# State space layer: head products and transposes issued singly between the wide products, and a new order of the steps around them

## The chip, the cores and the metric

The kernel runs on one core of one Trainium2 chip. The metric is the device time of one execution in microseconds (us); lower is better. The engines are TensorE (PE in the profile; PEld is its weight load), VectorE (DVE), ScalarE (ACT), GpSimd (POOL) and the DMA queue of SyncE (SP).

## The reference, cut to what matters

Four layers with residuals and layer norms around them: causal attention, a gated FFN, a state space layer (the subject here), a second gated FFN. The state space layer has a batch of 2 rows of 1024 tokens, width 512, 64 heads of 64 channels in 8 groups, and a state of 128 per channel:

```python
gate = proj[..., :I]; hbc = proj[..., I:I + CONV_DIM]; dt = proj[..., -H:]
xBC = silu(causal_conv4(hbc) + conv_bias)           # x, B, C
dA = exp(dt_p * A); dtx = dt_p[..., None] * x
state = state * dA + dtx * B_t;  y_t = state . C_t   # a scan over the tokens
y = y + x * D
yn = y * rsqrt(mean_group(y * y) + EPS) * norm_weight * silu(gate)
out = yn @ out_proj_w
```

## The kernel before, in words

The rows of the batch are a hardware loop over b. In it the phases attention, projection, FFN, time steps, state space (MAMBA in the code), FFN follow one another. The state space phase goes over 8 groups g of 8 heads each (`m_group`, one for each engine; the groups 1 to 6 are a hardware loop), and in a group over 8 chunks c of 128 tokens: 128 iterations `it` in all. The scan is done in chunks: within a chunk with products against a 128x128 decay matrix for each head, across chunks with a carried state. Each engine has its order written out by hand, and semaphores tie them together: an engine works strictly in its own order.

Every float32 operand of a large product is split into a high and a low part, and three products of the parts are added ("wide" products: 12 of 128x128 weights by 512 columns for each 128x512 output; helper `three`, L591 to L593; `features` is the projection of x, B, C for the convolution, `tokens` the gate's). Products of unsplit float32 (the heads', the state's) are two passes each.

TensorE's order in one iteration (L946 to L1017), with its bank in PSUM:

1. the four transposes of x for this chunk into bank 2 (L956), after `yt_ready` and `x_tm_ready` of the iteration before; ScalarE copies them to `x_tm` (L1239);
2. B's transpose and the product C by B into bank 3 (L961, L962). Bank 3 is also the out projection's, so these wait for `mo_used`: VectorE has added the last out projection to Y (`gather`, L1675, or L1673 for the first group);
3. the decays' sums, 4 products of 512 columns into banks 4 and 5 (L939, L940);
4. none, one or two projections for later chunks or the next group, 12 wide products each, into bank 0 or 1 in turn (even c: two; odd c: one; the last group has none from c = 4). Behind the first one stand the four transposes of the previous iteration's result yn into bank 2 (`turn_out`, L922);
5. the gate's projection, 12 wide, into the other of banks 0 and 1 (`bank_read` waits until that bank's last content was read by VectorE: `conv_ready`, signalled at L1647, for a projection);
6. the state's product into bank 6 (L997);
7. the 8 heads' products, decay matrix by xdt, 64 columns each, 2 passes: 16 in a row, into bank 7 (L1004), after `m_ready`, `pool_x`, `ss_ready`;
8. the out projection of the previous iteration into bank 3, 12 wide (`project_out`, L925), after `yt_ready`;
9. the update of the state, B by xw, into bank 6 (L1017), not for c = 7.

VectorE's order (L1696 to L1748): the masked decay matrix (L1659, L1662); for each projection the convolution's three taps (L1643, and for the second half of the tokens three small ones with the carry, L1640); after the first one yt_lo, the low part of the transposed result, which signals `yt_ready` (L1667); silu's product (L1652); the gate's product g_th (L1719); y's two additions (L1726 adds the heads' products from bank 7, L1729 adds the skip term xd and signals `y_ready`); at c = 1 and 6 the copies of `tables` (L1684, L1686); `gather` (L1675); the state's addition (L1744); the final yn (L1746).

ScalarE's order (L1234 to L1290): x_tm, b_tm, the decays' exp (L1218), for each projection the convolution's first tap (L1203) and silu's tanh (L1208), yt_hi behind the first (L1213), splits of weights, the gate's tanh (L1268), the eight scaled reads of bank 6 into yv (L1274), the square with its sum (L1277), splits of weights.

GpSimd's order (L2012 to L2059): xdt, xw, xd, splits of weights (L1993), the state's decay (L2032, after `inter_done` of the state's product), the two masked tables for the next chunk (L1999), the root (L2044, L2046), splits of weights.

Of the kernel before, what the change touches and what calls it, by code (L numbers as in the profile page):

```python
# [64 lines left out]
def build(nc, x, w_attn, qk_bias, bv, bo, w_ffn0, lr0, lr0_const, w_ffn1,  # L65
          w_mamba, w_dt, conv_par, dt_bias, a_log, d_skip, out):
    ctx = ExitStack()
    with ctx:
# [182 lines left out]
        pool_x = sem("pool_x")  # L251
# [334 lines left out]
        def _(pe):  # L586
# [173 lines left out]
            with pe.Fori(0, B) as b:  # L760
# [158 lines left out]
                def turn_out(it):  # L919
                    pe.wait_ge(yn_ready, START + it + 1)  # L920
                    for k in range(XT):
                        r = pe.transpose(bank[2][:, k * P:(k + 1) * P], yn[:, k * P:(k + 1) * P], ident[:])  # L922
                    r.then_inc(yt_done, 1)

                def project_out(it):  # L925
                    pe.wait_ge(yt_ready, START + it + 1)
                    for k in range(XT):
                        r = three(bank[3][:], lambda q: yt_hi[:, q, :], lambda q: yt_lo[:, q, :],
                                  lambda q: wy_hi[:, q, :], lambda q: wy_lo[:, q, :], k, k == 0, k == XT - 1)
                    r.then_inc(mo_done, 1)  # L930
# [12 lines left out]
                def m_group(g, first, last):  # L943
                    uses = m_uses(last)
                    at = 0
                    for c in range(TT):  # L946
# [5 lines left out]

                        pe.wait_ge(yt_ready, START + (it if start else it - 1))
                        pe.wait_ge(x_tm_ready, START + it)
                        for k in range(XT):
                            r = pe.transpose(bank[2][:, k * P:(k + 1) * P], xbc[s][:, k, ck], ident[:])  # L956
                        r.then_inc(xtr_done, 1)
# [9 lines left out]
                        turned = start  # L967
                        while uses[at][0] == "proj":
                            n = uses[at][1]
                            bank_read(g, at, uses)  # L970
                            ft = n % CT
                            if n < CT:
                                features(bank[at % 2][:], wx_hi[:, ft, :], wx_lo[:, ft, :], 1).then_inc(proj_done, 1)
                            else:
                                pe.wait_ge(m_split, b * (MG * W_PER_G) + (g + 1) * W_PER_G + (ft + 1))
                                features(bank[at % 2][:], wx_hi[:, ft, :], wx_lo[:, ft, :], 0).then_inc(proj_done, 1)
                            at += 1
                            if not turned:
                                pe.wait_ge(x_tm_ready, START + it + 1)
                                turn_out(it - 1)  # L980
                                turned = True
                        if start:
                            decays(it)
                        if not turned:
                            pe.wait_ge(x_tm_ready, START + it + 1)
                            turn_out(it - 1)

                        bank_read(g, at, uses)
                        if c == 0:
                            pe.wait_ge(m_split, b * (MG * W_PER_G) + g * W_PER_G + (CT + KT))  # L990
                        tokens(bank[at % 2][:], c, wg_hi, wg_lo).then_inc(gate_done, 1)
                        at += 1
# [14 lines left out]
                        if not start:  # L1007
# [37 lines left out]
                turn_out((b + 1) * (MG * TT) - 1)  # L1045
                norm_turn(b * 4 + 3, 3, (2, 3))
                project_out((b + 1) * (MG * TT) - 1)
# [7 lines left out]
        def _(act):  # L1055
# [87 lines left out]
            with act.Fori(0, B) as b:  # L1143
# [77 lines left out]
                def m_group(g, first, last):  # L1221
# [12 lines left out]
                    for c in range(TT):  # L1234
# [34 lines left out]
                        at += 1  # L1269
# [5 lines left out]
                        r.then_inc(inter_used, 1)  # L1275
                        act.wait_ge(y_ready, START + it + 1)
# [78 lines left out]
        def _(dve):  # L1355
# [170 lines left out]
            with dve.Fori(0, B) as b:  # L1526
# [161 lines left out]
                def m_group(g, first, last):  # L1688
# [7 lines left out]
                    for c in range(TT):  # L1696
# [27 lines left out]
                        dve.wait_ge(inter_used, START + it + 1)  # L1724
                        dve.wait_ge(intra_done, START + it + 1)
                        dve.tensor_tensor(yv[:], yv[:], bank[7], ALU.add)  # L1726
                        dve.drain()
                        dve.wait_ge(pool_x, START + it + 1)
                        dve.tensor_tensor(yv[:], yv[:], xd[:], ALU.add).then_inc(y_ready, 1)  # L1729
# [433 lines left out]
```

## Time and profile before

| | us |
|---|---|
| median of 3 runs (4126.3 to 4149.99) | 4126.65 |
| the profiled execution | 4139.81 |
| its span in the trace | 4138.1 |
| TensorE busy in the span | 3813.2 (92%) |
| VectorE busy | 2753.9 (67%) |
| ScalarE, GpSimd busy | 1706.8, 1816.2 |
| mean granted TensorE clock | 0.932 |

The times of the trace are us from the start of the span. A timeline's line is: start, duration, engine, line of the code, operation, what it writes and reads, count; in brackets the engine's idle time before it and what ended it. TensorE's records overlap (a product is recorded until its result is in PSUM), so its pace is read from one start to the next, not from the durations.

### The profile page before, as it was taken

What the parts mean: (1) busy time and instruction counts of PE and PEld (TensorE: products, weight loads), DVE (VectorE), ACT (ScalarE), POOL (GpSimd) and SP (SyncE); (2) the same over time, 40 slices, a digit from 0 to 9 for tenths busy, and PEclk for the clock granted to TensorE, in tenths of its full rate; (3) what the DMA queues carried; (4) which work ended last, traced back from release to release, by engine and by line L of the source; (5) the groups of instructions that cost most, each with busy time, mean ns of one, the idle gap of its engine ahead of it and who ended that gap; (6) DMA issues with size and microseconds to landing.
All of it is one profiled execution on the core that took longest, in us unless ns stands there. A gap on an engine that the chain in (4) does not pass through costs nothing.

```text
span 4138.1 us, 61540 instructions
## 1 busy us (share of the span) xinstructions
PE 3813.2 (92%) x18088; PEld 2789.9 (67%) x18088; DVE 2753.9 (67%) x5102; ACT 1706.8 (41%) x3555; POOL 1816.2 (44%) x1977
## 2 busy tenths in 40 slices
PE   7899899799999999979889998997999999999797
PEld 5444588577777777767654446875777777777676
DVE  5657455677777777764655655556777777777645
ACT  1434411455555555541214443114555555555412
POOL 1111444266655665553211124433565555655532
PEclk9867899899999999999987868998999999999998
DMA  3221111101010011011132111111011100110111
GB/s 81 47 35 23 63 45 33 33 26 37 28 33 20 26 36 28 23 36 54 38 68 44 32 50 34 46 32 39 21 37 33 28 26 20 36 33 18 47 43 36
DMA packets 84630, 151.95 MB, mean 37 GB/s; under 512 B 16488, under 2 KB 18616, under 8 KB 84432
## 3 DMA queue, kind: packets, MB, share of 16 engines
q1 hardware_dynamic: 82320, 145.38, 13.3%
q10 hardware_dynamic: 2112, 4.19, 0.3%
q8 instruction: 92, 1.51, 0.2%
q14 instruction: 106, 0.87, 0.1%
HBM read 119.37 MB, written 4.19 MB: 30 GB/s over the span
## 4 chain that ended last, share of the span: by engine, by line
PE 71%; issue 8%; DVE 8%; ACT 4%; DVEq 2%; POOL 2%; POOLq 1%; DMA 1%; SPq 1%; ACTq 1%; PEldq 0%; PEld 0%
PE banks L591 16%; PE banks L592 15%; PE banks L593 15%; PE banks L1004 4%; PE banks L841 4%; PE banks L822 3%; PE banks L799 3%; PE banks L997 2%; DVE conv L1643 2%; PE banks L1017 2%; DVEq L1646 1%; PE banks L939 1%; PE banks L940 1%; ACT conv L1203 1%; DVE conv L1640 1%
## 5 line engine op out<-in xcount | busy, mean ns | idle before, releaser
L1643 DVE SCALAR_TENSOR_TENSOR conv<-banks,cpar,conv 128x509 f32<-128x509 f32 (+2 forms) x576 | 428.6, 744 | 113.4 <-ACT conv L1203 98.3
L1169 ACT ACTIVATE probs<-banks 128x1024 f32<-128x1024 f32 (+3 forms) x384 | 298.7, 810 | 282.4 <-PE banks L822 281.4
L1967 POOL TENSOR_SCALAR_AFFINE_SELECT probs<-probs 128x256 f32<-128x256 f32 x256 | 104.3, 408 | 664.8 <-ACT probs L1169 664.4
L1430 DVE TENSOR_TENSOR Y<-banks,Y 128x512 f32<-128x512 f32 x368 | 253.3, 691 | 160.6 <-PE banks L593 160.1
L2032 POOL TENSOR_TENSOR state<-state,gt 128x512 f32<-128x512 f32 x112 | 133.5, 1192 | 505.4 <-PE banks L997 505.4
L591 PE MATMUL banks<-xhi,f_hi 128*128 128x512 f32 x800 | 325.0, 406 | 30.9 <-POOL f_lo L1846 16.6
L799 PE MATMUL banks<-stack_k,stack_q 48*128 48x512 f32 (+3 forms) x768 | 299.1, 466 | 39.0 <-DVE mx L1563 9.7
L591 PE MATMUL banks<-xhi,wx_hi 128*128 128x512 f32 x768 | 314.2, 409 | 6.8 <-DVE conv L1643 6.6
L592 PE MATMUL banks<-xhi,f_lo 128*128 128x512 f32 x800 | 320.3, 400 | 0.0
L593 PE MATMUL banks<-xlo,f_hi 128*128 128x512 f32 x800 | 320.2, 400 | 0.0
L592 PE MATMUL banks<-xhi,wx_lo 128*128 128x512 f32 x768 | 308.1, 401 | 0.0
L593 PE MATMUL banks<-xlo,wx_hi 128*128 128x512 f32 x768 | 307.8, 401 | 0.0
L1004 PEld LDWEIGHTS banks<-xdt,decay 128*128 128x128 f32 x2048 | 248.4, 192 | 68.6 <-issue 68.6
L1558 DVE CUSTOM_DVE_ANT_0 banks<-banks,mask_qk 128x128 f32<-128x128 f32 (+3 forms) x512 | 248.2, 501 | 64.8 <-PE banks L799 60.9
L822 PE MATMUL banks<-stack_q,stack_k 50*128 50x512 f32 (+3 forms) x768 | 272.4, 456 | 9.1 <-DMA stack_q<-mt_lo 7.7
L591 PE MATMUL banks<-wg_hi,xhi 128*128 128x512 f32 x512 | 221.8, 433 | 45.2 <-DVE conv L1643 41.9
L822 PEld LDWEIGHTS banks<-stack_q,stack_k 50*128 50x128 f32 x768 | 156.6, 232 | 153.9 <-issue 116.2
L1004 PE MATMUL banks<-xdt,decay 128*128 128x64 f32 x2048 | 242.8, 272 | 5.2 <-issue 2.6
L1844 POOL TENSOR_SCALAR f_hi<-f_raw 128x512 fp32r<-128x512 f32 x150 | 96.9, 646 | 321.9 <-PE banks L593 299.8
L1274 ACT ACTIVATE yv<-banks,gt 128x64 f32<-128x64 f32 x1024 | 223.8, 332 | 25.2 <-PE banks L997 25.2
L799 PEld LDWEIGHTS banks<-stack_k,stack_q 48*128 48x128 f32 x768 | 151.8, 221 | 121.0 <-DVE mx L1563 48.6
L1100 ACT CAST h_hi<-hf 128x512 fp32r<-128x512 f32 x100 | 62.3, 623 | 408.3 <-DVE hf L1415 408.3
(219 smaller groups left out, 10134.6 us busy)
## 6 DMA issues: line engine op xcount, KB each, us to landing
m_raw<-in_w_mamba SPq DMA_DIRECT2D x224, 256.0 KB, 2.6
f_raw<-in_w_ffn SPq DMA_DIRECT2D x50, 768.0 KB, 4.6
x_next<-in_x SPq DMA_DIRECT2D x6, 1024.0 KB, 8.6
stack_q<-X SPq DMA_DIRECT2D x96, 64.0 KB, 2.4
stack_k<-X SPq DMA_DIRECT2D x96, 64.0 KB, 2.5
wqk_raw<-in_w_attn SPq DMA_DIRECT2D x8, 512.0 KB, 3.5
stack_q<-part_hi SPq DMA_DIRECT2D x64, 64.0 KB, 2.4
stack_k<-part_hi SPq DMA_DIRECT2D x64, 64.0 KB, 2.5
```

The source lines that it names most:

```text
L591: pe.matmul(dst, a_hi(kt), w_hi(kt), start=first, stop=False)
L592: pe.matmul(dst, a_lo(kt), w_hi(kt), start=False, stop=False)
L593: return pe.matmul(dst, a_hi(kt), w_lo(kt), start=False, stop=last)
L799: pe.matmul(bank[RING_BANK[use]][:, 0:cols], stack_q[buf][base:base + ROWS, h, i * P:(i + 1) * P], stack_k[buf][base:base + ROWS, h, s * H ...
L822: r = pe.matmul(bank[h][:, at:at + w], stack_k[buf][base:base + ROWS + 2, h, j * P:(j + 1) * P], stack_q[buf][base:base + ROWS + 2, h, s * ...
L841: r = pe.matmul(bank[6][32 * h:32 * h + VW, lo:HALF], V[:, j, QUAD * t + h, :], probs[n % 2][:, h, at:at + w], start=j == 0, stop=j == CPH ...
L1004: r = pe.matmul(bank[7][:, h * MP:(h + 1) * MP], decay[:, h, :], xdt[:, h * MP:(h + 1) * MP], start=True, stop=True, skip_group_check=True)
L1169: act.activation(probs[n % 2][:, 2 * p:2 * p + 2, 0:w], banks[:, 2 * p:2 * p + 2, 0:w], ACT.Exp, scale=1.0 / HD ** 0.5).then_inc(exp_done[ ...
L1274: r = act.activation(yv[:, own], bank[6][:, own], ACT.Identity, scale=gt[:, EC, c, h:h + 1])
L1430: dve.tensor_tensor(Y[:, i, :], bank[6 + i % 2], Y[:, i, :], ALU.add).then_inc(f["dn_used"], 1)
L1558: dve.tensor_tensor_reduce(out=src, in0=src, in1=mask_qk[:, HALF - cols:HALF], scale=1.0, scalar=NEG, op0=ALU.add, op1=ALU.max, accum_out= ...
L1643: r = dve.scalar_tensor_tensor(out=rest, in0=src[:, 0:HALF - lag], scalar=cpar[:, o:o + 1], in1=rest, op0=ALU.mult, op1=ALU.add)
```

## The change

On TensorE:

- The heads' products are no longer a block of 16. They stand singly in the out projection: behind each of its wide products 0 to 7 one head (two passes).
- The four transposes of x for the next chunk stand behind wide products 8 to 11 of the out projection, where the next chunk is in the same half of the tokens ((c + 1) % 4 is not 0); otherwise, and for the first two chunks of the first group, they stay at the head of the iteration.
- The four transposes of yn stand behind wide products 8 to 11 of the first projection of the iteration, not behind the whole of it; without a projection (last group, c of 4 and more) behind products 0 to 3 of the gate's.
- The state's product (L997) is issued ahead of the gate's projection, not behind it.
- The heads wait for the new `xdt_ready` (xdt alone), and `pool_x` (xdt, xw and xd) is waited for by the state's update.

On ScalarE the eight reads into yv go ahead of the gate's tanh. On VectorE y's two additions go ahead of the gate's product, and a drain stands before yn. GpSimd signals `xdt_ready` behind xdt.

```diff
+                def wide(dst, a_hi, a_lo, w_hi, w_lo, between):
+                    n = 0
+                    for kt in range(KT):
+                        for a, w in ((a_hi, w_hi), (a_lo, w_hi), (a_hi, w_lo)):
+                            r = pe.matmul(dst, a(kt), w(kt), start=n == 0, stop=n == 3 * KT - 1)
+                            if n == 3 * KT - 1:
+                                r.then_inc(between["done"], 1)
+                            if n in between:
+                                between[n]()
+                            n += 1
+                def head(it, h):
+                    if h == 0:
+                        pe.wait_ge(m_ready, it + 1)
+                        pe.wait_ge(xdt_ready, it + 1)
+                        pe.wait_ge(ss_ready, START + it)
+                    r = pe.matmul(bank[7][:, h * MP:(h + 1) * MP], decay[:, h, :], xdt[:, h * MP:(h + 1) * MP],
+                                  start=True, stop=True, skip_group_check=True)
+                    if h == HPG - 1:
+                        r.then_inc(intra_done, 1)
...
-                        for k in range(XT):
-                            r = pe.transpose(bank[2][:, k * P:(k + 1) * P], xbc[s][:, k, ck], ident[:])
-                        r.then_inc(xtr_done, 1)
+                        if c % CPH == 0 or first and c == 1:
+                            pe.wait_ge(yt_ready, START + (it if start else it - 1))
+                            for k in range(XT):
+                                turn_x(it, c, k)
...
+                        turning = {} if start else {8 + k: lambda k=k: turn_out(it - 1, k) for k in range(XT)}
...
+                        bank_read(g, at, uses)
+                        heads = {h: lambda h=h: head(it, h) for h in range(HPG)}
+                        early = {n - 8: turn for n, turn in turning.items()}
+                        wide(bank[at % 2][:], lambda k: xhi[:, k, tok], lambda k: xlo[:, k, tok],
+                             lambda k: wg_hi[:, k, :], lambda k: wg_lo[:, k, :], {"done": gate_done, **early})
...
-                        pe.wait_ge(m_ready, it + 1)
-                        pe.wait_ge(pool_x, START + it + 1)
-                        pe.wait_ge(ss_ready, START + it)
-                        for h in range(HPG):
-                            r = pe.matmul(bank[7][:, h * MP:(h + 1) * MP], decay[:, h, :], xdt[:, h * MP:(h + 1) * MP],
-                                          start=True, stop=True, skip_group_check=True)
-                        r.then_inc(intra_done, 1)
...
-                            project_out(it - 1)
+                            ahead = (c + 1) % CPH != 0
+                            turns = {8 + k: lambda k=k: turn_x(it + 1, c + 1, k) for k in range(XT)} if ahead else {}
+                            project_out(it - 1, {**turns, **heads})
                         if c < TT - 1:
                             pe.wait_ge(inter_used, START + it + 1)
+                            pe.wait_ge(pool_x, START + it + 1)
@@ ScalarE
-                        act.wait_ge(gate_done, START + it + 1)
                         act.wait_ge(yn_ready, START + it)
-                        act.activation(g_th[:], bank[at % 2], ACT.Tanh, scale=0.5).then_inc(gate_th, 1)
...
                         r.then_inc(inter_used, 1)
+                        act.wait_ge(gate_done, START + it + 1)
+                        act.activation(g_th[:], bank[at % 2], ACT.Tanh, scale=0.5).then_inc(gate_th, 1)
@@ VectorE
+                        dve.wait_ge(inter_used, START + it + 1)
+                        dve.wait_ge(intra_done, START + it + 1)
+                        dve.tensor_tensor(yv[:], yv[:], bank[7], ALU.add)
+                        dve.drain()
+                        dve.wait_ge(pool_x, START + it + 1)
+                        dve.tensor_tensor(yv[:], yv[:], xd[:], ALU.add).then_inc(y_ready, 1)
                         dve.wait_ge(gate_th, it + 1)
                         dve.scalar_tensor_tensor(out=g_th[:], in0=g_th[:], scalar=1.0, in1=bank[at % 2],
                                                  op0=ALU.add, op1=ALU.mult).then_inc(gate_used, 1)
...
-                        dve.tensor_tensor(yv[:], yv[:], bank[7], ALU.add)
...
+                        dve.drain()
                         dve.wait_ge(rg_ready, it + 1)
@@ GpSimd
-                        pool.tensor_tensor(by_head(xdt[:]), by_head(x_tm[:]), per_head(gt[:, DTH, c, :]), ALU.mult)
+                        pool.tensor_tensor(by_head(xdt[:]), by_head(x_tm[:]), per_head(gt[:, DTH, c, :]), ALU.mult
+                                           ).then_inc(xdt_ready, 1)
```

## Rows read from the trace of the kernel before

The stretches of the first group run from one iteration's state product (L997) to the next one's; behind stretch and length stand the busy times of TensorE, its weight load, VectorE, ScalarE and GpSimd, then the granted clock.

**Rows 1.** Windows view: stretches that end at c = 1, 2, 4, 6, next 0

```profile
1469.14:1483.15 14.01, 14.01 (x73) 11.17 (x72) 9.29 (x13) 10.21 (x23) 10.26 (x11) 1.00 0.14 37
1483.15:1501.76 18.61, 17.31 (x84) 13.33 (x83) 15.10 (x29) 10.04 (x24) 12.90 (x12) 1.00 0.20 56
...
1515.77:1532.97 17.20, 17.08 (x85) 13.35 (x84) 14.98 (x19) 8.85 (x23) 10.77 (x10) 1.00 0.10 32
...
1546.97:1564.17 17.20, 17.09 (x85) 13.36 (x84) 11.74 (x17) 8.07 (x21) 7.17 (x8) 1.00 0.00 0
...
1578.17:1598.61 20.44, 17.99 (x82) 14.09 (x81) 16.21 (x26) 10.00 (x23) 9.23 (x9) 0.92 0.18 51
sum 129.47, PE 125.48 PEld 98.81 DVE 99.60 ACT 68.24 POOL 76.63; mean PE 15.69 PEld 12.35 DVE 12.45 ACT 8.53 POOL 9.58
```

**Rows 2.** Timeline of TensorE, iteration c = 5, from the state's product to the next decays

```profile
1546.97 1.02 PE L997 MATMUL banks<-state,xbc 128*128 128x512 f32 x2
1547.83 1.90 PE L1004 MATMUL banks<-xdt,decay 128*128 128x64 f32 x16
...
1552.39 1.02 PE L1017 MATMUL banks<-xw,b_tm 128*128 128x512 f32 x2
1553.25 0.60 PE L956 MATMUL banks<-ident,xbc 128*128 128x128 f32 x4
1553.69 0.27 PE L961 MATMUL banks<-ident,xbc 128*128 128x128 f32 x1
```

**Rows 3.** Timeline of TensorE's weight loads, same iteration, end of the heads

```profile
1549.51 0.19 PEld L591 LDWEIGHTS banks<-wy_hi,yt_hi 128*128 128x128 f32 x1
1549.62 0.19 PEld L592 LDWEIGHTS banks<-wy_hi,yt_lo 128*128 128x128 f32 x1
1549.85 0.19 PEld L593 LDWEIGHTS banks<-wy_lo,yt_hi 128*128 128x128 f32 x1
```

**Rows 4.** Timeline of VectorE, iterations c = 5, 6 and 7

```profile
1547.13 0.68 DVE L1667 TENSOR_TENSOR yt_lo<-banks,yt_hi 128x512 fp32r<-128x512 f32 x1
1547.73 0.68 DVE L1652 SCALAR_TENSOR_TENSOR xbc<-xbc,conv 128x512 f32<-128x512 f32 x1
...
1549.83 0.69 DVE L1726 TENSOR_TENSOR yv<-yv,banks 128x512 f32<-128x512 f32 x1 [0.82 <-ACT yv L1274]
1550.60 1.35 DVE L1729 TENSOR_TENSOR yv<-yv,xd 128x512 f32<-128x512 f32 x1
1552.59 0.69 DVE L1675 TENSOR_TENSOR Y<-banks,Y 128x512 f32<-128x512 f32 x1 [0.65 <-PE banks L593]
...
1569.39 0.60 DVE L1684 COPY gt<-tab 128x32 f32 x6
...
1582.00 0.69 DVE L1729 TENSOR_TENSOR yv<-yv,xd 128x512 f32<-128x512 f32 x1
```

**Rows 5.** Timeline of TensorE where it waits for bank 3, c = 1 of that group

```profile
1489.42 0.60 PE L956 MATMUL banks<-ident,xbc 128*128 128x128 f32 x4
1490.56 0.33 PE L961 MATMUL banks<-ident,xbc 128*128 128x128 f32 x1 [0.54 <-DVE Y L1675]
```

**Rows 6.** Timelines of TensorE and VectorE: a projection's end, yt_lo; c = 1, 3, 5

```profile
1479.92 0.60 PE L922 MATMUL banks<-ident,yn 128*128 128x128 f32 x4
...
1484.64 0.68 DVE L1667 TENSOR_TENSOR yt_lo<-banks,yt_hi 128x512 fp32r<-128x512 f32 x1
...
1512.54 0.60 PE L922 MATMUL banks<-ident,yn 128*128 128x128 f32 x4
...
1516.26 0.68 DVE L1667 TENSOR_TENSOR yt_lo<-banks,yt_hi 128x512 fp32r<-128x512 f32 x1
...
1543.75 0.60 PE L922 MATMUL banks<-ident,yn 128*128 128x128 f32 x4
```

**Rows 7.** Timeline of TensorE: the gate's first products behind a wait, next group's c = 0

```profile
1594.18 0.63 PE L591 MATMUL banks<-wg_hi,xhi 128*128 128x512 f32 x1 [2.10 <-DVE conv L1643]
1594.61 0.63 PE L592 MATMUL banks<-wg_hi,xlo 128*128 128x512 f32 x1
```

More of the change, by code:

```diff
@@ L250, in build @@
         au_ready, d_done, decay_ready, m_ready = (sem(n) for n in ("au_ready", "d_done", "decay_ready", "m_ready"))
-        pool_x = sem("pool_x")
+        pool_x, xdt_ready = sem("pool_x"), sem("xdt_ready")
         inter_done, inter_used, intra_done, y_ready = (
@@ new lines, in turn_out, with turn_x @@
+                def turn_out(it, k):
+                    if k == 0:
+                        pe.wait_ge(x_tm_ready, START + it + 2)
+                        pe.wait_ge(yn_ready, START + it + 1)
+                    r = pe.transpose(bank[2][:, k * P:(k + 1) * P], yn[:, k * P:(k + 1) * P], ident[:])
+                    if k == XT - 1:
+                        r.then_inc(yt_done, 1)
+                def turn_x(it, c, k):
+                    s, ck = c // CPH, slice(c % CPH * P, (c % CPH + 1) * P)
+                    if k == 0:
+                        pe.wait_ge(x_tm_ready, START + it)
+                    r = pe.transpose(bank[2][:, k * P:(k + 1) * P], xbc[s][:, k, ck], ident[:])
+                    if k == XT - 1:
+                        r.then_inc(xtr_done, 1)
@@ L926, in project_out @@
+                def project_out(it, between):
                     pe.wait_ge(yt_ready, START + it + 1)
[L927 to L930, printed above, removed]
+                    wide(bank[3][:], lambda q: yt_hi[:, q, :], lambda q: yt_lo[:, q, :],
+                         lambda q: wy_hi[:, q, :], lambda q: wy_lo[:, q, :], {"done": mo_done, **between})
@@ L970, in m_group @@
                             bank_read(g, at, uses)
[L971 to L974, printed above, removed]
+                            ft, half_ = n % CT, 1 if n < CT else 0
+                            if n >= CT:
                                 pe.wait_ge(m_split, b * (MG * W_PER_G) + (g + 1) * W_PER_G + (ft + 1))
-                                features(bank[at % 2][:], wx_hi[:, ft, :], wx_lo[:, ft, :], 0).then_inc(proj_done, 1)
+                            tok = slice(half_ * HALF, (half_ + 1) * HALF)
+                            wide(bank[at % 2][:], lambda k: wx_hi[:, ft, k * P:(k + 1) * P],
+                                 lambda k: wx_lo[:, ft, k * P:(k + 1) * P],
+                                 lambda k: xhi[:, k, tok], lambda k: xlo[:, k, tok], {"done": proj_done, **turning})
+                            turning = {}
                             at += 1
[L978 to L981, printed above, removed]
                         if start:
                             decays(it)
[L984 to L992, printed above, removed]
                         pe.wait_ge(state_ready, it + 1)
@@ L998, in m_group @@
                                   ).then_inc(inter_done, 1)
-                        pe.wait_ge(m_ready, it + 1)
-                        pe.wait_ge(pool_x, START + it + 1)
-                        pe.wait_ge(ss_ready, START + it)
-                        for h in range(HPG):
-                            r = pe.matmul(bank[7][:, h * MP:(h + 1) * MP], decay[:, h, :], xdt[:, h * MP:(h + 1) * MP],
-                                          start=True, stop=True, skip_group_check=True)
-                        r.then_inc(intra_done, 1)
-                        if not start:
+                        bank_read(g, at, uses)
+                        if c == 0:
+                            pe.wait_ge(m_split, b * (MG * W_PER_G) + g * W_PER_G + (CT + KT))
+                        tok = slice(c * P, (c + 1) * P)
+                        heads = {h: lambda h=h: head(it, h) for h in range(HPG)}
+                        early = {n - 8: turn for n, turn in turning.items()}
+                        wide(bank[at % 2][:], lambda k: xhi[:, k, tok], lambda k: xlo[:, k, tok],
+                             lambda k: wg_hi[:, k, :], lambda k: wg_lo[:, k, :], {"done": gate_done, **early})
+                        at += 1
+                        if start:
+                            for h in range(HPG):
+                                head(it, h)
+                        else:
                             if c == 1:
@@ L1044, in _ @@
                 norm_turn(b * 4 + 3, 3, (0, 1))
-                turn_out((b + 1) * (MG * TT) - 1)
+                pe.wait_ge(yn_ready, START + (b + 1) * (MG * TT))
+                for k in range(XT):
+                    r = pe.transpose(bank[2][:, k * P:(k + 1) * P], yn[:, k * P:(k + 1) * P], ident[:])
+                r.then_inc(yt_done, 1)
                 norm_turn(b * 4 + 3, 3, (2, 3))
-                project_out((b + 1) * (MG * TT) - 1)
+                project_out((b + 1) * (MG * TT) - 1, {})
                 leave(pe, b, MAMBA)
```

16 lines of the change are left out of this document (1 added, 15 removed).

## The prediction

> **What bounds the kernel now.** I read the page first: TensorE is busy 92% of the span, no other engine above 67%. Then the windows view, iteration by iteration. In one group [rows 1] the odd chunks take 14.0 us each, all of it TensorE's work. A second projection is 12 wide products at 0.232 us (the twelve of the out projection last from 1549.62, where the second of their weight loads starts [rows 3], to the start of the next product at 1552.39 [rows 2]: 2.77). So an even chunk's floor is 16.8, and 15.9 for c = 0, whose stretch lacks the state's update (0.86, L1017 to L956 in [rows 2]). Measured are 18.61, 17.20, 17.20 and 20.44 (c = 2, 4, 6 and the next 0 [rows 1]): of the group's 129.5 us some 7 are waits of TensorE. The reader is to see that here only two things can save time: TensorE's own work, or those 7 us, times 16 groups. Everything else can only add.
>
> **The singles.** The 16 passes of the heads take 1547.83 to 1549.62 in [rows 2, 3], 0.112 us each. Why is in rows 3: a weight load starts when the product before the one it is for starts. The load for the first wide product starts at 1549.51 and the next one only at 1549.62, 0.11 later, although the last head's product has just 64 columns; behind a wide product the loads are 0.23 apart. A pass therefore costs the larger of its own streaming and the next weight load: 0.232 for a wide one, 0.112 for a head's pass, 0.109 for a transpose (four in 0.44, L956 to L961 in [rows 2]). That sum has the same terms in any order. Between two wide products a head is still two passes, each followed by a load of 0.11 that only 64 columns cover: 2 x 0.112. Only its first load lies under a wide product, and in the block that is also so for the first head. So I cost the moves themselves at nothing: 8 x 0.224 = 1.79 and 8 x 0.109 = 0.87 per iteration before and after. Bounds: the trace has no single pass between two wide products into another bank. From below: all loads hidden, about 0.056 for each pass (half the block's pace, if the load hides the product today), 0.9 us less per iteration, 113 over 126 iterations. From above: one more exposed load per head, 8 x 0.11, as much more. I take nothing, since rows 3 are the nearest.
>
> The Trainium skill speaks otherwise: "TensorE: Matmul & The Clock Gate", step-by-step part, says that the queue pulls weight loads ahead of products in flight, so that the next tile's weights load while this tile's product runs. Taken freely it would hide every single load under a wide product; rows 3 show it only one product deep. Its result is rival A.
>
> **Added wait 1: bank 3, behind VectorE.** Let T be the start of the out projection. TensorE reaches B's transpose (bank 3) at T + 12 x 0.232 + 8 x 0.224 + 4 x 0.109 + 0.86 = T + 5.87. The last head's pass starts at T + 8 x 0.232 + 7 x 0.224 + 0.11 = T + 3.54 and lasts 0.27, to 3.81. The first addition of y starts 0.11 later (1549.73, where the L1004 row ends, to 1549.83 [rows 2, 4]), at 3.92; the second 0.77 later (1549.83 to 1550.60 [rows 4]) at 4.69; the gate's product, now behind it, 0.60 later (the pace of 0.68 us operations, 1547.13 to 1547.73 [rows 4]) at 5.29; gather at 5.89, and it takes 0.69: 6.58. With a weight load of 0.11 B's transpose starts at T + 6.69: a wait of 0.82. Before, gather only waited for the out projection (0.65 idle [rows 4]) and was through in the state's update and the four x transposes. Those transposes, now inside the out projection, no longer stand there as cover, and y's chain starts about 1.8 us later. Per group: five iterations (c = 0, 2, 3, 4, 5) at 0.82; c = 1 and 6 have the tables' copies ahead of gather, 0.60 more [rows 4]; c = 7 has no state update as cover, 0.86 more. Sum 4.10 + 2.84 + 1.68 = 8.6. Today's wait there goes off: at c = 1 0.70 (1489.42 + 0.44 to 1490.56 [rows 5]) and 0.5 at c = 7, 1.2 together. Net **+7.4 per group**.
>
> **Added wait 2: yt_ready ahead of the out projection.** In an odd chunk the heads' 1.8 us stood between the gate and the out projection; now it follows the gate at once. From the projection's end TensorE has one transpose, the state's product and the gate's: 0.11 + 0.86 + 2.78 = 3.75. yt_lo is behind the whole convolution on VectorE, which starts with the projection's end as before. At c = 1: 1479.92 + 3.75 = 1483.67, yt_lo ends 1485.32, plus a load 0.11: 1.76. c = 3: 1516.29 against 1517.05: 0.76. c = 5: 1547.50 against 1547.92: 0.42, and c = 7, which has a projection of the same kind, I take the same [rows 4, 6]. Even chunks have a second projection as cover. **+3.4 per group.** Behind this wait stand the heads and so y's chain, which moves along; wait 1, counted from T, stays whole.
>
> **Removed: the gate's wait for its bank.** The state's product (0.86) now fills time in which the gate waited for the convolution. It saves at most 0.86 where the wait was longer, or the wait: c = 2 0.86, c = 4 and c = 6 0.4 each (17.20 less 16.80 [rows 1]), c = 0 0.86 of 2.1 [rows 7]. **-2.5 per group.** At c = 0 the wait is also followed by products 0.43 apart instead of 0.23 (1594.18 to 1594.61 [rows 7], the lower level of the clock; 0.92 granted in [rows 1]). If the shorter wait spares that, up to 9 x 0.2 = 1.8 more; it stays in the range, since wait 2 at c = 1 could bring the clock down elsewhere.
>
> **Costed at nothing.** yn: gather at 6.58, the state's addition and GpSimd's root put yn's end near T + 8.5; its transposes come only behind nine wide products of the next projection, near T + 10. Without that cover each 0.1 us late would be 12 us in all. xdt_ready for pool_x, ScalarE's new order, the drain: each frees or holds something that is waited for over a us later. POOL's queue keeps its order.
>
> **Sum.** 7.4 + 3.4 - 2.5 = 8.3 us per group; of 16 groups the two first and two last lack parts (no project_out at the start, no projections from c = 4), so times 15.5: 128 us. The profiled execution took 4139.8, the median is 13.2 below it: 4126.65 + 128 = **4254 us**, 3% slower. Own range 4205 to 4310: y's second addition takes 0.69 to 1.35 [rows 4] when GpSimd works beside it (up to +40 if in half the iterations), and half of wait 2 could be covered (-27).
>
> **Rivals.** A: the loads hide. A single product between wide ones costs only its columns: the heads 113 us less, the transposes, if they too halve, 0.42 x 126 = 53 less. VectorE's waits stay: 4254 - 113 = 4141, or with the transposes and the clock spared at c = 0 (1.8 x 16 = 28) 4060, not slower. It decides from a head's price: at 0.11 instead of 0.22 the moves pay for all waits. For it: half the loads do now stand behind a wide product. Against: rows 3. Chance 0.15, 0.06 for the first time and 0.09 for the second. B: the waits do not add, since each gives VectorE time to catch up, and the clock's loss at c = 0 goes: half of 10.8 less 4.3, 1.1 per group, 4144. Against: both waits are counted from the product that starts VectorE's chain, so waiting does not shorten it. Chance 0.09. C: worse, the clock drops behind the longer wait at c = 1 (twelve products at +0.2, 2.4 per group) and y's addition collides with GpSimd: 4254 + 38 + 40 = 4330. Chance 0.08. The forecast keeps 0.68.
>
> A measurement of this kernel can tell about 1%, 41 us. Slower: the forecast and C, 0.76. Within 1%: A's first time and B, 0.15. Faster: A's second, 0.09. The range takes in B and A's first time and leaves out the two ends, A's second and most of C: 4090 to 4320.
>
> **What would show it.** Right: around each head two starts 0.11 apart and the next wide product another 0.11 later; L961 with about 0.8 us idle before it, released by L1675 (now behind L1719); the out projection's first product idle in odd chunks behind yt_lo; odd iterations near 15.3 instead of 14.0. Wrong: a head between wide products for 0.11 us in all (A), gather done before TensorE reaches bank 3, or yn's transposes waiting.

## The result, and the profile after

The changed kernel takes 4273.3 us (median of 4 runs, 4265.4 to 4291.01) against 4130.2 for the kernel before on the same chips: 1.033 times as long, 95% interval 1.030 to 1.037 (the two medians alone give 1.035). Forecast were 4254, 3% slower. The profiled executions' spans are 4275.9 and 4138.1 us, 138 apart.

The page of the kernel after, the parts that changed:

```profile
PE 3830.5 (90%) x18088; PEld 2758.9 (65%) x18088; DVE 2707.9 (63%) x5102; ACT 1688.9 (39%) x3555; POOL 1797.9 (42%) x1977
...
PE 62%; DVE 13%; issue 10%; POOL 5%; DVEq 4%; ACT 3%; POOLq 1%; DMA 1%; SPq 1%; ACTq 0%; PEldq 0%; PEld 0%
```

The same 18088 products are busy for about as long as before (3830.5 us against 3813.2), while the span grew by 138: TensorE does the same work and waits more. The chain that ended last passes through VectorE for 13% of the span; it was 8%.

The windows view of one group of the kernel after, from one state product to the next (all eight stretches, the first from c = 0 to c = 1; the columns are those of the rows from before, and the third number from the end is the granted clock):

```profile
1507.93:1524.53 16.60, 14.48 (x72) 10.81 (x71) 11.87 (x20) 8.41 (x20) 9.21 (x10) 1.00 0.15 41
1524.53:1544.56 20.03, 17.28 (x85) 13.16 (x84) 13.40 (x28) 11.70 (x26) 15.17 (x15) 1.00 0.25 71
1544.56:1559.89 15.33, 14.54 (x72) 10.83 (x72) 13.21 (x20) 6.43 (x17) 8.26 (x9) 1.00 0.06 17
1559.89:1578.60 18.71, 17.30 (x85) 13.36 (x84) 12.68 (x20) 9.28 (x23) 10.61 (x11) 1.00 0.11 29
1578.60:1593.42 14.82, 14.29 (x72) 10.91 (x71) 11.07 (x14) 6.60 (x18) 7.84 (x9) 1.00 0.06 18
1593.42:1611.55 18.13, 17.31 (x85) 13.18 (x84) 11.39 (x16) 8.42 (x22) 8.07 (x9) 1.00 0.00 0
1611.55:1626.96 15.41, 14.28 (x72) 10.87 (x71) 11.76 (x22) 5.97 (x17) 8.91 (x9) 1.00 0.00 0
1626.96:1645.09 18.13, 16.44 (x84) 12.93 (x82) 12.04 (x17) 10.42 (x25) 7.50 (x9) 1.00 0.11 29
sum 137.16, PE 125.92 PEld 96.05 DVE 97.41 ACT 67.23 POOL 75.58; mean PE 15.74 PEld 12.01 DVE 12.18 ACT 8.40 POOL 9.45
```

This group takes 137.2 us where it took 129.5 [rows 1]. The trace has fourteen such groups from state product to state product; together they are 118 us longer than before, 8.4 each, and the last group of each of the two batch rows adds 11 in sum. So 129 of the 138 us lie in the state space phase. The other 9 lie outside it and were not taken apart; from run to run those parts differ by as much (the time ahead of the first state product is 819 to 839 us in the twelve traces). The stretches are not one to one with those of before: the gate's projection now stands behind the state's product, so its wait counts in the next stretch. Priced at 0.232 us (a wide product or a decays' product), 0.428 (a pass of the state's product or update), 0.112 (a head's pass) and 0.109 (a transpose), the group's products need 122.3 us (4 x 14.0 + 3 x 16.8 + 15.9) in both orders: 7.2 us of waiting and slow clock before, 14.9 after.

Timeline of TensorE in the iteration c = 4 of this group of the kernel after ([rows 2] show c = 5; both are among the five iterations for which the prediction has a wait of 0.82):

```profile
1582.30 0.40 PE L924 MATMUL banks<-wy_hi,yt_hi 128*128 128x512 f32 x1
1582.53 0.33 PE L955 MATMUL banks<-xdt,decay 128*128 128x64 f32 x2
1582.67 0.48 PE L924 MATMUL banks<-wy_hi,yt_lo 128*128 128x512 f32 x1
1582.99 0.33 PE L955 MATMUL banks<-xdt,decay 128*128 128x64 f32 x2
1583.13 0.48 PE L924 MATMUL banks<-wy_lo,yt_hi 128*128 128x512 f32 x1
...
1586.53 0.27 PE L945 MATMUL banks<-ident,xbc 128*128 128x128 f32 x1
1586.56 0.48 PE L924 MATMUL banks<-wy_hi,yt_lo 128*128 128x512 f32 x1
1586.87 0.27 PE L945 MATMUL banks<-ident,xbc 128*128 128x128 f32 x1
...
1587.32 1.02 PE L1046 MATMUL banks<-xw,b_tm 128*128 128x512 f32 x2
1588.88 0.33 PE L992 MATMUL banks<-ident,xbc 128*128 128x128 f32 x1 [0.53 <-DVE Y L1707]
```

One wide product with one head is 0.46 us (1582.67 to 1583.13), one with a transpose 0.34 (1586.53 to 1586.87): 0.232 and 0.224, 0.232 and 0.109 would be 0.456 and 0.341. Standing singly is worth nothing and costs next to nothing. The timeline of the weight loads at the same place shows why:

```profile
1582.30 0.42 PEld L955 LDWEIGHTS banks<-xdt,decay 128*128 128x128 f32 x2
1582.64 0.19 PEld L924 LDWEIGHTS banks<-wy_hi,yt_lo 128*128 128x128 f32 x1
1582.76 0.43 PEld L955 LDWEIGHTS banks<-xdt,decay 128*128 128x128 f32 x2
```

The first load for a head starts with the wide product (1582.30); the load for the next wide product starts only 0.34 later (0.23 and 0.11), and the next head's 0.12 behind that. So one load of each head lies under a wide product, and the others are paid at 0.11 each.

Behind the out projection and the state's update, B's transpose, ready to go at 1587.32 + 0.86 = 1588.18, starts at 1588.88, released by the gather.

VectorE's timeline beside it:

```profile
1586.17 0.69 DVE L1752 TENSOR_TENSOR yv<-yv,banks 128x512 f32<-128x512 f32 x1 [2.68 <-PE banks L955]
1586.93 0.69 DVE L1755 TENSOR_TENSOR yv<-yv,xd 128x512 f32<-128x512 f32 x1
1587.54 0.68 DVE L1757 SCALAR_TENSOR_TENSOR g_th<-g_th,banks 128x512 f32<-128x512 f32 x1
1588.14 0.69 DVE L1707 TENSOR_TENSOR Y<-banks,Y 128x512 f32<-128x512 f32 x1
```

With T = 1582.30 the prediction had these at 1586.22, 1586.99, 1587.59 and 1588.19. Before, VectorE stood idle 1.40 us ahead of y's first addition in this iteration and 0.82 in c = 5 [rows 4]; now it is 2.68 and 3.20, and everything behind it is late.

Timeline of TensorE in the iteration c = 1 of the same group, where the out projection waits:

```profile
1528.00 0.39 PE L924 MATMUL banks<-wg_lo,xhi 128*128 128x512 f32 x1
1530.02 0.47 PE L924 MATMUL banks<-wy_hi,yt_hi 128*128 128x512 f32 x1 [1.62 <-POOL wy_lo L2026]
1530.33 0.33 PE L955 MATMUL banks<-xdt,decay 128*128 128x64 f32 x2
```

What it waits for there, from the timelines of GpSimd and VectorE:

```profile
1527.31 2.58 POOL L2026 TENSOR_TENSOR wy_lo<-m_raw,wy_hi 128x512 fp32r<-128x512 f32 x2 [0.50 <-ACT wy_hi L1224]
...
1529.20 0.67 DVE L1699 TENSOR_TENSOR yt_lo<-banks,yt_hi 128x512 fp32r<-128x512 f32 x1
```

### The profile page after: what moved, and what is told of

Same layout as the page of the kernel before. It is cut to its first block, busy times and chain, and to the rows that moved or that the text cites. A ratio compares the mean times of both kernels' runs of the same rounds, so it can differ in the third digit from the quotient of the medians.

```text
span 4275.9 us, 61588 instructions
## 1 busy us (share of the span) xinstructions
PE 3830.5 (90%) x18088; PEld 2758.9 (65%) x18088; DVE 2707.9 (63%) x5102; ACT 1688.9 (39%) x3555; POOL 1797.9 (42%) x1977
## 4 chain that ended last, share of the span: by engine, by line
PE 62%; DVE 13%; issue 10%; POOL 5%; DVEq 4%; ACT 3%; POOLq 1%; DMA 1%; SPq 1%; ACTq 0%; PEldq 0%; PEld 0%
PE banks L924 20%; PE banks L591 8%; PE banks L592 7%; PE banks L593 7%; PE banks L955 4%; PE banks L841 4%; PE banks L799 3%; PE banks L822 3%; DVE conv L1675 2%; DVE yv L1752 2%; DVEq L1678 2%; POOL wy_lo L2026 2%; DVE conv L1672 1%; ACT conv L1235 1%; DVE yv L1755 1%
## 5 line engine op out<-in xcount | busy, mean ns | idle before, releaser
L955 PEld LDWEIGHTS banks<-xdt,decay 128*128 128x128 f32 x2048 | 393.6, 193 | 55.1 <-DVE decay L1694 5.4
L2078 POOL TENSOR_SCALAR rg<-ss 128x1 f32<-128x1 f32 x128 | 25.7, 201 | 777.2 <-ACT banks L1309 777.2
L955 PE MATMUL banks<-xdt,decay 128*128 128x64 f32 x2048 | 341.0, 250 | 6.8 <-DVE decay L1694 4.5
L924 PE MATMUL banks<-xhi,wx_hi 128*128 128x512 f32 x720 | 300.7, 418 | 0.0
L924 PE MATMUL banks<-xlo,wx_hi 128*128 128x512 f32 x720 | 295.9, 411 | 0.0
L1752 DVE TENSOR_TENSOR yv<-yv,banks 128x512 f32<-128x512 f32 x128 | 88.0, 687 | 325.8 <-PE banks L955 324.2
L924 PE MATMUL banks<-wy_hi,yt_hi 128*128 128x512 f32 x512 | 240.1, 469 | 48.3 <-POOL wy_lo L2026 26.4
L1309 ACT ACTIVATE banks<-yv 128x512 f32<-128x512 f32 x128 | 77.0, 602 | 518.6 <-DVE yv L1755 518.6
L924 PE MATMUL banks<-wg_hi,xhi 128*128 128x512 f32 x512 | 240.3, 469 | 25.6 <-DVE conv L1675 25.6
L924 PE MATMUL banks<-wy_hi,yt_lo 128*128 128x512 f32 x512 | 245.4, 479 | 0.0
```

Source lines behind the costliest of these rows:

```text
L924: r = pe.matmul(dst, a(kt), w(kt), start=n == 0, stop=n == 3 * KT - 1)
```

## The experiments

Two theories stood against each other at first: the loss is waiting that the new order makes (theory 1), or the singles themselves, or VectorE's and ScalarE's new orders, cost the time (rivals 1 and 2; they are numbered apart from the prediction's A, B and C). The kernel before, run beside them, had medians from 4130 to 4144 us; so ratios are compared, not times.

**Heads in a block again**, all else as changed:

```diff
-                        if start:
-                            for h in range(HPG):
-                                head(it, h)
-                        else:
+                        for h in range(HPG):
+                            head(it, h)
+                        if not start:
...
-                            project_out(it - 1, {**turns, **heads})
+                            project_out(it - 1, turns)
```

> The changed kernel with its heads' products in one block again, ahead of the out projection; all else as changed (the state's product ahead of the gate's, VectorE's and ScalarE's new orders, transposes singly). Theory 1 (the loss is waiting: the singles start y's chain on VectorE late, and the block that covered yt_ready is gone): both waits fall to about what they were, the gain of the state's product (2.5 us per group) stays, so about 4130 - 40 = 4090 us, B's transpose waits 2 us per group or less. Rival 1 (a single product between wide ones is dearer than one in a block): also fast, so this run does not speak against it. Rival 2 (VectorE's and ScalarE's new orders cost the time): stays near 4270.

4103 us, ratio to before 0.991 (0.987 to 0.994): faster than before, by the 40 us that theory 1 gives. The heads' single places carry the whole loss and hid a gain. Rival 2 falls: both new orders are in this kernel. Rival 1 is not touched by this run; the pace of 0.46 us for a wide product and a head, in the timeline above, speaks against it. The row of the products by form that stands for B's transpose shows 29.6 us idle, against the changed kernel's 96.2:

```profile
L992 PE MATMUL banks<-ident,xbc 128*128 128x128 f32 x128 | 40.5, 316 | 29.6 <-DVE Y L1706 26.0 <-DVE Y L1704 3.5
```

The same view of the kernel before, the rows of the gate, the out projection and B's transpose:

```profile
L591 PE MATMUL banks<-wg_hi,xhi 128*128 128x512 f32 x512 | 221.8, 433 | 45.2 <-DVE conv L1643 41.9
L591 PE MATMUL banks<-wy_hi,yt_hi 128*128 128x512 f32 x512 | 212.4, 415 | 0.8 <-POOL wy_lo L1993 0.8
L961 PE MATMUL banks<-ident,xbc 128*128 128x128 f32 x128 | 37.0, 289 | 14.0 <-DVE Y L1675 12.0 <-DVE Y L1673 2.0
```

And of the kernel after the change:

```profile
L955 PE MATMUL banks<-xdt,decay 128*128 128x64 f32 x2048 | 341.0, 250 | 6.8 <-DVE decay L1694 4.5 <-issue 2.3
L924 PE MATMUL banks<-wg_hi,xhi 128*128 128x512 f32 x512 | 240.3, 469 | 25.6 <-DVE conv L1675 25.6
L924 PE MATMUL banks<-wy_hi,yt_hi 128*128 128x512 f32 x512 | 240.1, 469 | 48.3 <-POOL wy_lo L2026 26.4 <-DVE yt_lo L1699 21.9
L992 PE MATMUL banks<-ident,xbc 128*128 128x128 f32 x128 | 42.4, 331 | 96.2 <-DVE Y L1707 84.7 <-DVE Y L1705 11.6
```

In the last column stands TensorE's idle time ahead of the group. The two added waits are the last two rows, 48.3 us where it was 0.8 and 96.2 where it was 14.0; the gate's wait for the convolution fell from 41.9 to 25.6.

**Singles alone**, in the kernel before:

```diff
-                        for h in range(HPG):
-                            r = pe.matmul(bank[7][:, h * MP:(h + 1) * MP], decay[:, h, :], xdt[:, h * MP:(h + 1) * MP],
-                                          start=True, stop=True, skip_group_check=True)
-                        r.then_inc(intra_done, 1)
...
-                            project_out(it - 1)
+                            project_out(it - 1, {h: lambda h=h: head(it, h) for h in range(HPG)})
```

> The kernel before with one part of the change alone: the heads' products singly behind wide products 0 to 7 of the out projection; transposes, the state's product and the other engines' orders as before. Theory 1: VectorE's y chain starts 1.8 us later and the out projection waits for yt_ready and the weights' split, some 5 us per group: 4130 + 85 = 4215 us, with the singles' own pace at 0.456 us for a wide product and a head. Rival 1 (dearer singles): the same sign, but the pace shows more than 0.46 and the waits stay as before. Rival 2 (the new orders cost it): 4130.

Ratio 1.023 (1.019 to 1.027), 4235 us, some 93 us over before; expected were 85. Its waits view:

```profile
PE banks L930 <- POOL wy_lo L2004: 30.7, 16, 2.9
PE banks L591 <- POOL wg_lo L2004: 29.9, 14, 2.1
PE banks L976 <- DVE Y L1686: 25.1, 38, 0.9
```

Here the out projection waits 16 times, once in each group, for the split of its weights, and the gate 14 times for the split of its own (at c = 0, where it waited 2.1 us for the convolution before [rows 7]). B's transpose waits 38 times for the gather; that wait is small here. VectorE's old order has the gate's product ahead of y's additions, and the x transposes still stand ahead of B's; how much each of the two does was not separated in this run. A wide product with a head takes 0.46 us here too, so rival 1 falls; rival 2, which expected no loss, falls as well.

**Gather ahead of the gate's product**, in the changed kernel:

```diff
+                        if not start:
+                            gather(it - 1, (c - 1) % TT, first)
                         dve.wait_ge(gate_th, it + 1)
...
-                        if not start:
-                            gather(it - 1, (c - 1) % TT, first)
```

> The changed kernel with VectorE's gather (the addition that frees bank 3) ahead of the gate's product and of the tables' copies, right behind y's two additions. Theory 1: gather ends 0.60 us earlier in each iteration, 1.2 at c = 1 and 6; some 4.3 us per group come back, 4273 - 70 = 4203 us, and the idle time ahead of B's transpose falls to about a quarter. Rival 1 (dearer singles) and rival 2 in the form that y ahead of the gate costs: no change, 4273.

Ratio 1.020 (1.016 to 1.023) where the changed kernel has 1.033, 4220 us. A reordering of VectorE by 0.6 us gives back 1.4%, about 56 us of the 70 expected; no product was touched. The idle time ahead of B's transpose falls from 96 to 11 us, so the wait goes almost wholly, but not all of it comes back: the gate now waits 17.9 us for the split of its weights, which it did not do in the changed kernel, and at c = 1 the granted clock is 0.92 in all fourteen whole groups, against four in the changed kernel (some 1.6 us each, see the gate's bank below).

**Bank 3's products behind the decays**, in the changed kernel:

```diff
+                        if not start:
+                            decays(it)
                         pe.wait_ge(mo_used, START + (it if start else it - 1))
                         pe.wait_ge(bc_ready, START + it)
                         pe.transpose(bank[3][:, 0:P], xbc[s][:, XT, ck], ident[:])
...
-                        if not start:
-                            decays(it)
```

> The changed kernel with B's transpose and C by B (bank 3) behind the four decay products instead of ahead of them, so that 0.93 us of other work covers the gather. Theory 1: the wait of 0.82 goes in the five plain iterations, what is left is 0.5 to 0.8 at c = 1, 6 and 7; b_tm and the masked matrix come 0.9 later, which nothing waits for; some 4.5 us per group come back, about 4200 us. Rival 1: no change, 4273. Rival 3 (VectorE's chain bounds the iteration, so any wait taken away comes back later in it): no change or under 20 us.

Ratio 1.018 (1.013 to 1.023), 4217 us. The wait for the gather, 0.7 us in a plain iteration, was real and removable by cover: ahead of B's transpose 12 of the 96 us idle are left. As in the run before, the gate waits for the split of its weights (21.4 us), and the clock is lower at c = 1 in ten of fourteen groups. Rivals 1 and 3 expected nothing here.

**VectorE's old order** (gate's product ahead of y's additions), in the changed kernel: the six lines of y's additions moved back behind `gate_used`.

> The changed kernel with VectorE's old order: the gate's product ahead of y's two additions, all else as changed. The gate's product is ready long before the heads are through, so ahead of them it costs nothing. Theory 1: y's additions start where they did, gather 0.60 us earlier, about 3.6 us per group back: 4273 - 58 = 4215 us. Rival (the new order on VectorE was needed for yn to be in time): slower than 4273.

Ratio 1.020 (1.017 to 1.023), 4224 us: the same as moving the gather. B's transpose waits 29 us in all, with the x transposes in their new place. That part of the change was a loss by itself as long as the heads come late.

**The gate first again**, in the changed kernel: the state's product moved back behind the gate's projection.

> The changed kernel with the state's product behind the gate's projection again. Theory 1: the gate's wait for its bank comes back, 2.5 us per group as the prediction's third term has it: 4273 + 40 = 4313 us. Rival (the state's product only moves a wait about, since GpSimd or VectorE bounds the group): 4273.

Ratio 1.049 (1.046 to 1.052), 4337 us: 1.6% more than the changed kernel, some 64 us for the 40 expected. The gate's wait for the convolution is 67.0 us here against 25.6; it now waits at c = 4 and 6 too, some 0.5 us each. The clock at c = 0, spared in the changed kernel, falls again in seven of the fourteen whole groups, as it did in nine before the change [rows 7]:

```profile
PE banks L992 <- DVE Y L1708: 84.5, 110, 1.4
PE banks L924 <- DVE conv L1676: 67.0, 60, 2.4
```

**The state's product first, alone**, in the kernel before: only this block moved ahead of the gate's projection.

> The kernel before with one part of the change alone: the state's product ahead of the gate's projection, everything else as before. Theory 1: the third term by itself, 2.5 us per group: 4130 - 40 = 4090 us. Rival: ScalarE still has its tanh ahead of the eight reads, nothing is gained, 4130.

Ratio 0.994 (0.992 to 0.996), 4112 us of 9 runs: a gain of 26 us, not 40; in the profiled execution a middle group takes 126.6 us instead of 129.4, but the last groups gain nothing. A group of the kernel before that keeps its clock at c = 0 takes 128.3, so of the 2.8 us 1.8 are waiting and the rest is the clock. Of the 40 us that the heads in a block gained, 26 are this part; what the single transposes, the new orders and `xdt_ready` add was not taken apart.

**yt_hi and yt_lo ahead of the convolution**, in the changed kernel:

```diff
-                            before_conv(bank[at % 2], p0 + n, n, s1)
-                            if not turned_yet:
+                            own_turn = not turned_yet
+                            if own_turn:
                                 turned_hi(it - 1)
                                 turned_yet = True
+                            before_conv(bank[at % 2], p0 + n, n, s1)
+                            if own_turn:
                                 more_splits(c)
...
-                            convolve(bank[at % 2], p0 + n, n, s1)
                             if not turned:
                                 turned_lo(it - 1)
                                 turned = True
+                            convolve(bank[at % 2], p0 + n, n, s1)
```

> The changed kernel with yt_hi on ScalarE and yt_lo on VectorE ahead of the projection's convolution instead of behind it, so that yt_ready comes 3 us earlier and the out projection need not wait for it. If the waits simply added, 2.3 us per group (wait 2 without c = 1, where the weights' split comes as late) would come back: 4273 - 37 = 4236 us. But the convolution ends about 1.2 us later (0.58 for the copy, 0.60 for the subtraction), and with two projections the gate waits for that: theory 1 says the wait moves to the gate's bank and the time stays within 15 us of 4273.

Ratio 1.031 (1.026 to 1.035), 4265 us, within 10 of the changed kernel and not to be told from it. Its waits show the move, against those of the changed kernel in the rows by form above:

```profile
PE banks L992 <- DVE Y L1709: 84.4, 110, 1.4
PE banks L924 <- DVE conv L1677: 36.4, 58, 1.6
...
PE banks L924 <- POOL wy_lo L2028: 26.4, 16, 1.7
```

The 21.9 us of waiting for yt_lo are gone and the gate's wait for the convolution grew from 25.6 to 36.4, with twice as many of them (58, where the changed kernel has 28). What remains of wait 2 is the weights' split at c = 1.

**Both covers for bank 3, heads singly**: the edits of the third and fourth run together.

> The changed kernel, heads singly, with both edits against wait 1 at once: gather ahead of the gate's product and bank 3's products behind the decays. Each alone gave back about 4.3 us per group. Theory 1: both remove the same wait, so together hardly more than one of them, 4205 us; what is left over the kernel with its heads in a block (4062 with bank 3 late) is wait 2, the out projection behind yt_ready and the weights' split, some 8 us per group. Rival 3 (they add): 4140.

Ratio 1.013 (1.008 to 1.018), 4191 us: 2.0% below the changed kernel, where either edit gave 1.4 and 1.5. B's transpose has no idle time left in the row by form (L994, 0.0), so what remains are the other waits:

```profile
PE banks L924 <- POOL wy_lo L2026: 28.3, 15, 2.1
PE banks L924 <- DVE yt_lo L1699: 27.1, 45, 1.8
PE banks L924 <- POOL wg_lo L2026: 21.5, 14, 1.5
```

**Heads in a block, bank 3 late**: the edits of the first and fourth run together, the kernel that the experiments point to.

> The changed kernel with the heads' products in a block and bank 3's products behind the decays: both edits that gave time back. Theory 1: no wait for bank 3 is left, an odd chunk is back at 14.0 us or near it, an even one near 16.8; 125 us per group against 129.4 before, 4130 - 70 = 4060 us, the fastest of all. Rival 3 (a chain on VectorE or GpSimd is bound next, so that the two do not add): 4100, no better than the block alone.

Ratio 0.983 (0.980 to 0.986), 4062 us: the fastest of all, 1.7% below the kernel before. Five of the eight stretches of one of its groups, the first from c = 0 to c = 1, and the sum of all eight:

```profile
1444.80:1460.70 15.90, 14.31 (x72) 10.86 (x72) 12.91 (x20) 8.54 (x20) 9.25 (x10) 1.00 0.20 48
1460.70:1477.70 17.00, 17.00 (x85) 13.29 (x84) 14.14 (x28) 11.63 (x26) 15.66 (x15) 1.00 0.28 78
1477.70:1492.00 14.30, 14.30 (x72) 10.81 (x71) 12.95 (x19) 6.34 (x17) 7.46 (x8) 1.00 0.04 10
1492.00:1508.80 16.80, 16.80 (x85) 13.30 (x84) 13.21 (x21) 9.30 (x23) 11.39 (x12) 1.00 0.14 39
1508.80:1522.90 14.10, 14.10 (x72) 10.99 (x71) 10.74 (x14) 6.62 (x18) 8.57 (x9) 1.00 0.06 19
...
sum 125.10, PE 123.51 PEld 96.49 DVE 99.31 ACT 67.26 POOL 76.22; mean PE 15.44 PEld 12.06 DVE 12.41 ACT 8.41 POOL 9.53
```

TensorE is busy in the whole of the last four; of 125.1 us only 2.8 are over the floor of 122.3, most of them in the first stretch, 15.9 instead of 14.0, which holds the gate's wait at c = 0. No run has the heads in a block and VectorE's old order, so whether y's additions first are worth anything in this kernel is not shown.

## Why the prediction was right, point by point

**The singles cost nothing: right.** A wide product with a head takes 0.46 us and one with a transpose 0.34, as the weight loads priced them. The step that carried it was [rows 3]. Rival A falls with that pace; where its first form had 0.34 for a wide product and a head, the trace has 0.46. The Trainium skill ("TensorE: Matmul & The Clock Gate", step-by-step part) says that the next tile's weights load while this tile's product runs. The trace agrees one product deep: a load is pulled ahead of one product and no further (0.34 us from a head's first load to the next wide product's).

**Wait 1, bank 3: right in mechanism, somewhat large in size.** The chain T + 3.92, 4.69, 5.29, 5.89 came out 0.05 us early at each step in c = 4. B's transpose waited 0.7 (ready 1588.18, started 1588.88) for the 0.82 forecast. One step was read from a row that did not show it: the 0.11 us from the heads' end to y's first addition was taken from [rows 4], where that addition was released by ScalarE's yv and not by the heads. The kernel after shows the same 0.11, with the heads as the releaser (1586.06 to 1586.17), so the figure held by luck. Over the run the idle time ahead of B's transpose grew by 82 us, from 14 to 96; counted from start to start, 0.70 for the 0.53 of the row, it is an estimate of 100, where 7.4 x 15.5 = 115 were forecast.

Three experiments took the wait away in three ways, 67 to 85 of its 96 us, and gave back 54 to 62; the two covers together took all of it and gave 2.0%, 83 us. The rest came up elsewhere. With both covers the gate waits 21.5 us for the split of its weights, where it waited for nothing of the kind, yt_lo costs 27.1 for 21.9, the state's product waits 8.2 for 3.0, and the gate's wait for the convolution fell to 8.9 from 25.6. And the clock falls at c = 1 in more groups: in 14, 10 and 8 of the fourteen whole ones with the gather early, bank 3 late and both, against four in the changed kernel.

**Wait 2, the out projection: right in size, in part wrong in cause.** At c = 1 the wait was 1.8 us (1528.00 + 0.23 to 1530.02) as forecast (1.76), but what ended it was GpSimd's split of wy (L2026), which the prediction had not priced; it ended at 1529.89 (1527.31 and 2.58) and yt_lo at 1529.87 (1529.20 and 0.67), so either alone would have held it. One of the two causes was not seen; that they end 0.02 us apart, so that the forecast's size fits, is luck. Of the 48.3 us idle, 26.4 are put down to the split, all at c = 1, and 21.9 to yt_lo, in the other odd chunks. So bringing yt_lo forward alone cannot help at c = 1, and elsewhere it moved the wait to the gate, as the run showed.

**The gate's bank, -2.5 per group: right in sign; the size depends on the kernel around it.** Alone it gave 26 us where 39 were forecast; put back in the changed kernel it cost 64, with the clock. The possible extra, the clock at c = 0, came true: the last stretch has 1.00 granted in all fourteen whole groups of the changed kernel, where nine of fourteen were lower before (0.92 in [rows 1]). Part of it was given back at c = 1, as the prediction left open: in some groups the clock falls there instead (the windows view of such a group of the kernel after, c = 1 to 2):

```profile
1385.80:1407.40 21.60, 18.84 (x85) 14.53 (x84) 13.39 (x28) 11.70 (x26) 15.16 (x15) 0.92 0.23 64
```

That is 1.6 us more than the same stretch at full clock, 20.03, and it happened in 5 of the 16 groups.

**The sum.** Forecast were +8.3 us per group, times 15.5: 128 us. Measured are 8.4 in the mean of the fourteen whole groups (7.7 in the pair shown, whose group before is one with the lower clock), and 129 in the state space phase; the 9 us more of the whole kernel lie outside it. So the sum fits better than its terms, of which wait 1 is too large by the estimate above. Rival B (the waits do not add) did not decide the whole, but is what limits each single repair. Of rival C the clock came true in 5 of the 16 groups. Its collision did not: y's second addition took 0.69 us in each of the 128 iterations of the changed kernel, where it took 1.12 in the mean before. The 40 us held ready for it in the range were not needed. The costs at nothing held: TensorE's waits for yn, whose cover was to be over a us, are 0.5 us in all ahead of the single transposes, and were 11.0 before.

## What to carry to other kernels

Before small products are spread between large ones, price each by the larger of its own columns and the next weight load. Where a load is pulled only one product deep, as here (0.46 us for a wide product and a head in any place), the order of the same products changes nothing on TensorE, and all that moves is when their last result is ready. A block of small products in front of a long one is cheap cover: it gives the next engine's chain its input early and gives a late operand time to arrive. When a wait is removed, look at who is second, and at the clock in the stretch behind it: here each of three edits took away 67 to 85 us of the same wait and gave back 54 to 62. The best kernel came from the order that starts VectorE's chain early together with cover for the shared bank.

## What the runs showed of the hardware that was not expected

A wait of TensorE and the lower clock behind it do not go by the wait's length alone. Waits of 0.5 to 1.4 us ahead of bank 3, one in each iteration, left the granted clock at 1.00 from c = 2 on in all fourteen whole groups. In the changed kernel a wait of 1.62 us at c = 1 was followed by the lower level in 5 of 16 groups and not in the others: the group with 0.92 granted shows the same wait of 1.62 us as the one with 1.00. With the gather early the waits there are 1.6 to 2.1 us and the clock fell in 14 of 14 whole groups; with VectorE's old order they are as long, 1.6 to 2.1, and it fell in 2 of 14. What decides is left open.

VectorE's addition of two operands in SBUF (y's second one) took up to 1.36 us before, over 1 us in 92 of 128 iterations, and 0.69 in all of them after the change, though none of its operands changed. That GpSimd's work beside it is the cause, as the prediction has it, was not tested.
